# A dropout, dense adjacency matmul and layer norm: 4 MB loads of 32 KB rows, grouped stores, tapered last loads

## The reference

```python
keep = (u >= 0.1).astype(x.dtype)
x_drop = x * keep / (1.0 - 0.1)
h = x + jnp.matmul(adj, x_drop)
m = jnp.mean(h, axis=-1, keepdims=True)
v = jnp.var(h, axis=-1, keepdims=True)
out = (h - m) / jnp.sqrt(v + 1e-5)
```

## Time and profile before

| | |
|---|---|
| median of 3 runs | 664.6 us (664.34 to 664.64) |
| span of the profiled execution | 662.4 us |
| TensorE busy | 512.4 us (77%) |
| VectorE busy | 54.9 us (8%) |
| ScalarE busy | 17.1 us (3%) |
| DMA | 274.88 MB, mean 415 GB/s |

### The profile page before, as it was taken

One profiled execution on the slowest core, in us unless ns is written; L12 is line 12 of the kernel. 1 busy time (PEld: TensorE's weight loads), 2 busy tenths in 40 slices (PEclk: granted clock), 3 DMA queues, 4 the chain that ended last, 5 costly groups with the idle time before them and its releaser, 6 DMA issues.

```text
span 662.4 us, 5938 instructions
## 1 busy us (share of the span) xinstructions
PE 512.4 (77%) x2304; PEld 150.5 (23%) x2304; DVE 54.9 (8%) x105; ACT 17.1 (3%) x36; POOL 0.9 (0%) x8
## 2 busy tenths in 40 slices
PE   0877778787877878778787887878778787788886
PEld 0222122121211212112122221222122221221443
DVE  2471001010000101001010010101001010010100
ACT  0002000000000000000000000000000000000000
POOL 0000000000000000000000000000000000000000
PEclk9999999999999999999999999999999999999999
DMA  8999999999999999999999999999999999999995
GB/s 344 419 422 420 423 421 422 422 421 422 422 423 423 421 423 422 422 423 423 421 422 424 421 423 422 423 422 422 423 421 423 423 421 423 423 421 422 419 423 225
DMA packets 40617, 274.88 MB, mean 415 GB/s; under 512 B 4512, under 2 KB 6688, under 8 KB 7968
## 3 DMA queue, kind: packets, MB, share of 16 engines
q1 hardware_dynamic: 37008, 268.45, 97.4%
q10 hardware_dynamic: 3600, 6.29, 2.5%
HBM read 272.63 MB, written 2.10 MB: 415 GB/s over the span
## 4 chain that ended last, share of the span: by engine, by line
DMA 65%; SPq 28%; PE 5%; issue 2%; DVE 0%; ACT 0%; DVEq 0%
DMA piece<-adj 57%; SPq L102 28%; DMA piece<-adj_last 8%; PE acc L139 5%; SPq L109 0%; PE folded L154 0%; ACT sums_T L215 0%; ACT std L218 0%; DVE squares L281 0%; DVE y L277 0%; DVE square_sum L284 0%; DVE rows L292 0%; DVE rstd L287 0%; SPq L106 0%; DVEq L291 0%
## 5 line engine op out<-in xcount | busy, mean ns | idle before, releaser
L139 PE MATMUL acc<-piece,xdrop 128*64 128x512 f32 (+1 forms) x2176 | 496.7, 580 | 145.6 <-DMA piece<-adj 120.8
L139 PEld LDWEIGHTS acc<-piece,xdrop 128*64 128x64 f32 x2176 | 134.9, 136 | 494.7 <-DMA piece<-adj 311.7
L277 DVE SCALAR_TENSOR_TENSOR y<-folded,x_sb 128x256 f32<-128x256 f32 (+1 forms) x17 | 7.0, 409 | 573.1 <-PE folded L154 573.1
L215 ACT COPY sums_T<-acc 128x512 f32<-128x512 f32 (+1 forms) x17 | 9.5, 560 | 516.7 <-PE acc L139 516.6
L154 PEld LDWEIGHTS folded<-fold,sums_T 128*128 128x128 f32 x128 | 15.6, 191 | 13.1 <-issue 11.3
L154 PE MATMUL folded<-fold,sums_T 128*128 128x64 f32 x128 | 17.9, 281 | 0.5 <-ACT sums_T L215 0.5
L292 DVE TENSOR_TENSOR rows<-y,rstd 128x256 f32<-128x256 f32 (+1 forms) x17 | 7.0, 410 | 1.6
L281 DVE TENSOR_TENSOR squares<-y 128x256 f32<-128x256 f32 (+1 forms) x17 | 7.0, 409 | 0.6
L284 DVE TENSOR_REDUCE square_sum<-squares 128x4 f32<-128x256 f32 (+1 forms) x17 | 6.9, 404 | 0.6
L218 ACT ACTIVATE std<-square_sum,eps 128x4 f32<-128x4 f32 (+1 forms) x17 | 5.1, 297 | 68.9 <-DVE square_sum L284 68.9
L262 DVE SCALAR_TENSOR_TENSOR u_sb<-u_sb,x_sb 128x1024 f32<-128x1024 f32 x4 | 4.9, 1226 | 23.0 <-DMA u_sb<-u 23.0
(11 more groups left out here) (4 smaller groups left out, 0.4 us busy)
## 6 DMA issues: line engine op xcount, KB each, us to landing
piece<-adj SPq DMA_DIRECT2D x240, 1024.0 KB, 27.1
piece<-adj_last SPq DMA_DIRECT2D x15, 1024.0 KB, 27.4
x_sb<-x ACTq DMA_DIRECT2D x4, 512.0 KB, 16.9
u_sb<-u ACTq DMA_DIRECT2D x4, 512.0 KB, 20.2
out<-rows ACTq DMA_DIRECT2D x15, 128.0 KB, 7.0
piece<-adj_last SPq DMA_DIRECT2D x2, 512.0 KB, 26.0
out<-rows ACTq DMA_DIRECT2D x2, 64.0 KB, 4.8
```

What stands on the lines that cost most here:

```text
L139: last = nc.tensor.matmul(acc[i][D * h:D * h + D, 0:cols], xdrop[:, k, :], piece[:, b, :], start=(k < 2), stop=(k >= NB - 2))
L215: nc.scalar.copy(sums_T[:, i, 0:nj * P], acc[i][:, 0:nj * P]).then_inc(sums_copied, 1)
L277: nc.vector.scalar_tensor_tensor(out=y[:, i, 0:nj, :], in0=folded[i][:, 0:nj, :], scalar=1.0 / (1.0 - P_DROP), in1=x_sb[:, bass.ds(block0, ...
```

## The change

- `SLOTS` goes from 16 to 4, with four times as many blocks in each buffer: a wide load is 4 MB, its row 32 KB. The buffers hold 16 MB as before.
- x and u are loaded whole (2 MB, rows of 16 KB) by SyncE, ahead of the first piece. u lands in `xdrop` itself and is masked and centred in place; the mask waits for both loads.
- The last two narrow chunks (8 MB each, 64 blocks of 1 KB a row) come in 15 loads, by the table `PARTS`: 26, 6, 15 and 17 blocks for the first, and 14, 11, 7, 2, 8, 6, 5, 4, 3, 2, 2 for the second.
- `rows` becomes a buffer for the whole output. ScalarE stores after every fourth chunk 16 blocks (4 KB a row), before the last chunk 14 blocks, and at the end the last 2: five stores in place of 17. VectorE no longer waits for stores.
- In the last narrow chunk 0.9 x is put into PSUM by a matmul with `lift` (0.9 times the identity) ahead of the last loads, and the two folds accumulate on it (`lifted`), so that PSUM holds 0.9 y. The copy is split in two halves of 128 columns, with the first fold beside the second copy. The mean square is then taken for one block by ScalarE (`Square` with a sum) and for the other by VectorE (`bn_stats`, `bn_aggr`); eps is scaled by 0.81 to fit. y, its squares and their sum are no longer instructions of their own there.
- Four small tiles (`lift`, `eps_lifted`, `stats`, `moments`) and three small POOL operations for the first two are added, and x_sb has to be centred before the `lift` matmuls.

The diff, cut to what the steps of the prediction touch:

```diff
-SLOTS = 16
+SLOTS = 4
...
-TAIL_PARTS = (4, 4)
...
-XQ = 4
-XB = NB // XQ
+GROUP = 4
 P_DROP = 0.1
+KEEP = 1.0 - P_DROP
...
+PARTS = ((26, 6), (15, 17), (14, 11, 7), (2, 8, 6, 5, 4, 3, 2, 2))
...
+        lifted = pb("lifted", [P, LAST_J, COLS])
...
+        parts = [(s, sum(sizes[:n]), size) for s, sizes in enumerate(PARTS) for n, size in enumerate(sizes)]
...
+            sp.dma_start(x_sb[:, :, :], x[:, :, :]).then_inc(x_in, 16)
+            sp.dma_start(xdrop[:, :, :], u[:, :, :]).then_inc(u_in, 16)
...
-            for s in range(SLOTS):
-                sp.wait_ge(piece_used, (CHUNKS - 2) * SLOTS + s + 1)
-                if s < SLOTS - 1:
-                    sp.dma_start(narrow[s], adj_last[s, :, :, :]).then_inc(piece_in[s], 16)
-                else:
-                    for n, (b, size) in enumerate(last_parts):
-                        sp.dma_start(narrow[s][:, b:b + size, :],
-                                     adj_last[s, :, b:b + size, :]).then_inc(part_in[n], 16)
+            for n, (s, b, size) in enumerate(parts):
+                if b == 0:
+                    sp.wait_ge(piece_used, (CHUNKS - 2) * SLOTS + s + 1)
+                sp.dma_start(narrow[s][:, b:b + size, :], adj_last[s, :, b:b + size, :]).then_inc(part_in[n], 16)
         @block.gpsimd
         def _(pool):
...
+            nc.gpsimd.affine_select(out=lift[:, :], in_=lift[:, :], compare_op=ALU.not_equal, fill=KEEP, base=0,
+                                    pattern=[[-1, P]], channel_multiplier=1).then_inc(lift_ready, 1)
...
-                    h = b % 2
+                    h = k % 2
...
-                for n in range(LAST_SLOTS):
-                    s = m * LAST_SLOTS + n
-                    if s < SLOTS - 1:
-                        pe.wait_ge(piece_in[s], 16 * CHUNKS)
-                        products(i, narrow[s], n * LAST_PB, LAST_PB, LAST_COLS)
-                    else:
-                        for part, (b, size) in enumerate(last_parts):
-                            pe.wait_ge(part_in[part], 16)
-                            products(i, narrow[s][:, b:b + size, :], n * LAST_PB + b, size, LAST_COLS)
-                    if n == 0:
+                for n, (s, b, size) in enumerate(parts):
+                    if s // LAST_SLOTS != m:
+                        continue
+                    k0 = (s % LAST_SLOTS) * LAST_PB + b
+                    pe.wait_ge(part_in[n], 16)
+                    last = products(i, narrow[s][:, b:b + size, :], k0, size, LAST_COLS)
+                    if k0 + size == NB:
+                        last.then_inc(narrow_done, 1)
+                    if k0 == 0:
                         fold_rows(c - 1, 1 - i, nj=LAST_J if m else J)
-            fold_rows(FINAL, FINAL % 2, nj=LAST_J)
+                        if c == FINAL:
+                            pe.wait_ge(lift_ready, 1)
+                            pe.wait_ge(x_centred, SLOTS)
+                            for j in range(LAST_J):
+                                nc.tensor.matmul(lifted[:, j, 0:D], lift[:, :], x_sb[:, NB - LAST_J + j, :],
+                                                 start=True, stop=False)
+            i = FINAL % 2
+            pe.wait_ge(sums_copied, FINAL + 1)
+            nc.tensor.matmul(lifted[:, 0, 0:D], sums_T[:, i, 0:P], fold[:, :],
+                             start=False, stop=True).then_inc(folded_ready, 1)
+            pe.wait_ge(half_copied, 1)
+            nc.tensor.matmul(lifted[:, 1, 0:D], sums_T[:, i, P:2 * P], fold[:, :],
+                             start=False, stop=True).then_inc(folded_ready, 1)
...
-            for q in range(XQ):
-                for dst, src in ((x_sb, x), (u_sb, u)):
-                    act.dma_start(dst[:, q * XB:q * XB + XB, :], src[:, q * XB:q * XB + XB, :]).then_inc(x_in[q], 16)
...
+            def store(c, first, blocks):
                 act.wait_ge(rows_ready, c + 1)
-                act.dma_start(out[:, bass.ds(block0, nj), :], rows[:, i, 0:nj, :]).then_inc(stored[i], 16)
-            def wide(c, i, again=True):
-                step(c, i, c * SLOTS + SLOTS, c * J, again)
+                act.dma_start(out[:, bass.ds(first, blocks), :], rows[:, bass.ds(first, blocks), :]).then_inc(stored, 16)
...
+            store(3, 0, GROUP * J)
+            with act.Fori(1, CHUNKS // GROUP - 1) as g:
+                for n in range(GROUP):
+                    wide(g * GROUP + n, n % 2)
+                store(g * GROUP + (GROUP - 1), g * (GROUP * J), GROUP * J)
+            for n in range(GROUP - 1):
+                wide(CHUNKS - GROUP + n, n % 2)
+            act.wait_ge(narrow_done, 1)
+            act.wait_ge(folded_ready, CHUNKS - 2)
+            nc.scalar.copy(sums_T[:, 1, 0:LAST_COLS], acc[1][:, 0:LAST_COLS]).then_inc(sums_copied, 1)
+            spread(CHUNKS - 1, LAST_J)
+            store(CHUNKS - 1, NB - GROUP * J, GROUP * J - LAST_J)
+            i = FINAL % 2
+            act.wait_ge(narrow_done, 2)
+            act.wait_ge(folded_ready, FINAL - 1)
+            nc.scalar.copy(sums_T[:, i, 0:P], acc[i][:, 0:P]).then_inc(sums_copied, 1)
+            nc.scalar.copy(sums_T[:, i, P:2 * P], acc[i][:, P:2 * P]).then_inc(half_copied, 1)
+            act.wait_ge(folded_ready, FINAL + 1)
+            nc.scalar.activation(squares[:, 0, :], lifted[:, 0, 0:D], ACT.Square, scale=D ** -0.5,
+                                 accum_out=moments[:, 0, 1:2]).then_inc(last_var0, 1)
+            act.wait_ge(last_var0, 1)
+            act.wait_ge(last_var1, 1)
+            nc.scalar.activation(std[:, 0:LAST_J], moments[:, :, 1], ACT.Sqrt,
+                                 bias=eps_lifted[:, :]).then_inc(std_ready, 1)
+            store(FINAL, NB - LAST_J, LAST_J)
+            act.wait_ge(stored, 16 * (CHUNKS // GROUP + 1))
...
+            dve.wait_ge(x_in, 16)
+            dve.wait_ge(u_in, 16)
+            for q in range(SLOTS):
+                nc.vector.scalar_tensor_tensor(out=xdrop[:, quarter(q), :], in0=xdrop[:, quarter(q), :], scalar=P_DROP,
...
-                    dve.wait_ge(stored[i], stores)
...
+            dve.wait_ge(folded_ready, FINAL + 2)
+            nc.vector.bn_stats(stats[:, :], lifted[:, 1, 0:D]).then_inc(last_stats, 1)
+            dve.wait_ge(last_stats, 1)
+            nc.vector.bn_aggr(moments[:, 1, :], stats[:, :]).then_inc(last_var1, 1)
+            dve.wait_ge(std_ready, FINAL + 1)
+            nc.vector.reciprocal(rstd[:, 0:LAST_J], std[:, 0:LAST_J]).then_inc(rstd_ready, 1)
+            dve.wait_ge(rstd_ready, FINAL + 1)
+            nc.vector.tensor_tensor(rows[:, NB - LAST_J:NB, :], lifted[:, :, 0:D], per_row(rstd, LAST_J),
+                                    ALU.mult).then_inc(rows_ready, 1)
```

More of the change, by code:

```diff
@@ L94, in graph_layernorm @@
         rows_ready = sem("rows_ready")
-        stored = [sem(f"stored{i}") for i in range(2)]
+        stored = sem("stored")
         block = ctx.enter_context(nc.Block())
@@ L219, in step, with wide @@
                                      scale=1.0 / D).then_inc(std_ready, 1)
+            def wide(c, i, again=True):
+                act.wait_ge(piece_used, c * SLOTS + SLOTS)
+                if again:
+                    act.wait_ge(folded_ready, c - 1)
+                nc.scalar.copy(sums_T[:, i, :], acc[i][:, :]).then_inc(sums_copied, 1)
+                spread(c)
+            def store(c, first, blocks):
                 act.wait_ge(rows_ready, c + 1)
-                act.dma_start(out[:, bass.ds(block0, nj), :], rows[:, i, 0:nj, :]).then_inc(stored[i], 16)
@@ L240, in _ @@
-            for i in range(2):
-                act.wait_ge(stored[i], 16 * ((FINAL + 2 - i) // 2))
+            wide(2, 0)
+            wide(3, 1)
+            store(3, 0, GROUP * J)
[6 more added lines that the diff above has]
+            act.wait_ge(narrow_done, 1)
@@ L245, in quarter @@
             def quarter(q):
-                return slice(q * XB, q * XB + XB)
+                return slice(q * PB, q * PB + PB)
             def centre(out, in_, q, which, ready):
-                n = which * XQ + q + 1
+                n = which * SLOTS + q + 1
                 nc.vector.reduce_sum(node_sum[:, which, quarter(q)], in_[:, quarter(q), :],
@@ L287, in normalise @@
                 nc.vector.reciprocal(rstd[:, 0:nj], std[:, 0:nj]).then_inc(rstd_ready, 1)
-                if stores is not None:
-                    dve.wait_ge(stored[i], stores)
                 dve.wait_ge(rstd_ready, c + 1)
-                nc.vector.tensor_tensor(rows[:, i, 0:nj, :], y[:, i, 0:nj, :], per_row(rstd),
+                nc.vector.tensor_tensor(rows[:, bass.ds(block0, nj), :], y[:, 0:nj, :], per_row(rstd, nj),
                                         ALU.mult).then_inc(rows_ready, 1)
@@ L300, in _ @@
                     c = t * 2 + i
[L301 to L305 removed]
+                    normalise(c, i, c * J)
+            normalise(CHUNKS - 2, 0, (CHUNKS - 2) * J)
+            normalise(CHUNKS - 1, 1, NB - J, nj=LAST_J)
+            dve.wait_ge(folded_ready, FINAL + 2)
```

(1 more changed line is left out.)

78 lines of the change are left out of this document (34 added, 44 removed).

## The result

The changed kernel takes 649.1 us (648.9 to 649.2) against 664.5 us: a ratio of 0.9768, 95% interval 0.9753 to 0.9784, so 2.3% faster. A fourth run of it took 1019.0 us at a granted clock of 1.00 and is left out: no profile shows why, and none of the 69 runs of the experiments came near it. The forecast was 647.8 us with a range of 643 to 657. The profiled execution has a span of 647.3 us, where the forecast had 645.6.

What follows compares the result with a forecast made beforehand. The prediction took the DMA engines' byte stream and the tail behind it to bound the kernel. Savings of 15.0 + 1.1 + 0.7 = 16.8 us gave a 645.6 us span, 647.8 us with the median's 2.2 us; range 643 to 657.

Steps and rivals of the forecast that it cites:

- What bounds the kernel: Whole span: the DMA engines moving 275 MB at 422 GB/s, then the tail after the last byte.
- Term 1: Loads and stores: 28,800 fewer packets, 1,800 an engine at 8.4 ns each, save 15.0 us (11.7 to 18.7).
- rivals 1 and 2: Large rows: cut into 8 KB packets or rate-limited, 659.8 us, chance 0.10; only half the packet price goes, 655.3 us, 0.09.
- engine time as packets x h + bytes x p: Two DMA queues: solved for h, 8.4 ns a packet, and p, 0.0373 ns a byte.
- Term 2: Last matmuls: only 2 blocks stand behind the last byte, 0.7 us instead of 1.8, saving 1.1 us (0 to 1.2).
- it is through with them: Tapered last loads: TensorE has finished all earlier blocks when the last 2 land, at 0.215 us a block against 0.31.
- Term 3: Chain from the last copy's start to the store's issue: 2.4 us instead of 3.1, saving 0.7 us.
- What costs nothing: x and u first, four buffers, grouped stores, `lift` matmuls and other engines' changes: no time lost.
- x and u first: Start on SyncE's queue: TensorE starts at about 22 us instead of 15.45, covered by the buffers, at no cost.
- Rival 3, the clock: TensorE drops to half clock in 2.6 us waits between pieces; with eight slow blocks a piece, 696 us; chance 0.05.
- its point of decision: Rival 3, the clock: a piece has 9.7 us; four slow blocks (8.8 us) cost nothing, the seventh is first to matter.
- The wait it feeds on is gone by then: Argument against Rival 3, the clock: once slow blocks lengthen a piece, TensorE's wait between pieces has vanished.

Runs made afterwards that it cites:

- runs 1 to 3: Changed kernel with loads in 8 KB rows, 662.5 us; with eight buffers and 16 KB rows, 653.8; with 8 KB rows and each load issued as four, 662.6.
- run 8: Changed kernel with a store of 1 KB rows after every chunk again, in place of the grouped stores: 648.8 us.
- run 1: Changed kernel with the same 4 MB loads, each partition's part cut into four rows of 8 KB: 662.5 us.
- run 9: Changed kernel with the last two chunks in even loads (32, 32, four of 8, then 8, 8, 8, 4, 4) instead of tapered ones: 649.4 us.
- run 12: Changed kernel with the mean square of both last blocks taken by ScalarE, one Square behind the other, none on VectorE: 648.7 us.
- run 6: Changed kernel with two idle matmuls more behind each piece, filling 0.9 us of TensorE's wait: 649.1 us.
- run 7: Changed kernel with x and u back in four quarters each on ScalarE's queue: 652.3 us.
- slots2: Changed kernel with two buffers and loads of 8 MB, rows of 64 KB: 666.0 us.

## Why the prediction held, step by step

**What bounds the kernel** was right: the DMA share is 1.00 over 500 us and the tail is what is left.

**Term 1, forecast 15.0 us, measured 14.3.** The mechanism and the steady rate were right (432 forecast, 431 read), and rivals 1 and 2 fall with it: no row was cut, and the whole price went, not half. What was wrong is the unit. The step "engine time as packets x h + bytes x p" gave all packets one price of 8.4 ns. By runs 1 to 3 a row that is loaded costs 9.3 ns and a report under 1, and by run 8 the rows of the small stores cost nothing. The 9.3 ns on the 1,440 rows that run 1 puts back make 13.4 us; the forecast had 1,440 x 8.4 = 12.1 for them and 3.0 for the other 360 packets, of which about 0.9 came. Of those, 64 are rows of x, u and the narrow loads, 0.6 us at 9.3 ns; 96 are rows of stores and 200 are reports; 0.3 us stay open. Two errors against each other, then, and that the sum came out so close is luck. The rule of 3 cycles in "DMA: Bandwidth & Descriptors", section "Why small descriptors are slow", of the Trainium skill, an estimate of 3.5 ns by the page's clock, would have made this term 1,800 x 3.5 = 6.3 us; the sum was right not to go by it: the runs show 9.3.

**Term 2, forecast 1.1 us, measured 0.6.** The step "it is through with them" was right, and two blocks took the 0.67 us that were priced. What was mis-sized is the start: the last two blocks began 0.5 us behind the last bytes, and the step had 0.05. As a part of the whole the taper is worth 0.3 us, since without it the loads end earlier (run 9).

**Term 3, forecast 0.7 us, measured 0.3.** Copies and folds came nearly as priced (1.09 us to the start of `bn_stats` for 1.0), and so did `bn_stats` (0.23 for 0.25) and `bn_aggr` (0.18 for 0.17). The hand-over from `bn_aggr` to the root took 0.42 us where 0.05 had been put; that is the term that was mis-sized, and run 12 gets it back.

**What costs nothing.** Four buffers: right, by the DMA share and run 6. The grouped stores: right that they cost nothing, but neither do single ones, so the rows saved there bring nothing. x and u first: right as a sum and incomplete as a reason. The step said that the buffers cover a late start. It did not ask what 32 KB rows would do to a load with 4 KB rows on another queue, which run 7 prices at 3.2 us.

**Rival 3, the clock.** Its mechanism appeared, in some pieces and with about four slow blocks ((8.62 - 7.09) / 0.43 = 3.6), and its point of decision held: a piece of 8.8 us against 9.7 costs nothing. The section on HAM oscillation in "TensorE: Matmul & The Clock Gate" of the Trainium skill tells of a fall before every burst; the clock line here agrees in part, with 18 of 59 pieces. "The wait it feeds on is gone by then" did not keep it away; it cost nothing since no piece took over 8.8 us of its 9.7. In slots2 the mechanism has a price.

The span was missed by 1.7 us: 0.7 in term 1, 0.5 in term 2, 0.4 in term 3 and 0.1 behind the store's issue. The median stands 1.8 us above the span now and stood 2.2 above it before, which leaves the 1.3 us.

## What to carry to other kernels

In a kernel that streams at the DMA engines' limit, count the rows that each engine loads: here every one cost 9.3 ns beside its bytes, whatever the size of the load it belonged to. Before making rows longer, look at what shares the engines with them, since a short-rowed load on another queue then waited a long row for each of its own; put what is needed first ahead of the stream, on the same queue. Larger loads also hold their buffer longer: four buffers had slack for a half clock, while two of the same total size lost 17 us against them.
